# Sums over both experts of a pair in 128x64 tiles, banks in turns, and nine routing steps, in the last mixture-of-experts layer

## The chip, the cores and the metric

One core of a Trainium2 chip runs the whole program in one launch. The metric is the device time in microseconds; the median over three runs of the kernel before is 643.99 us (643.71 to 646.05). Engines are named as in the profile: PE is the matrix engine, PEld its weight load, DVE the vector engine, ACT the scalar engine, POOL the GpSimd engine, SP the engine that issues most DMAs.

## The reference

A batch of 128 images (64 x 1000) is cut into 82 overlapping patches each; a linear map and a gelu give 82 tokens of 64 channels. Two layers follow, each an attention and a mixture of experts, both with layer norm and a residual. The change is in the last mixture of experts, which has 8 experts and takes the best two of each token:

```python
logits = tokens.astype(jnp.float32) @ router_w.astype(jnp.float32).T
probs = jax.nn.softmax(logits, axis=-1)
rw, re = jax.lax.top_k(probs, TOP_K)
rw = rw / jnp.maximum(rw.sum(-1, keepdims=True), 1e-12)
combine = jnp.zeros((N, E)).at[jnp.arange(N)[:, None], re].set(rw)
out = tokens
for e in range(E):
    h = jax.nn.gelu(tokens @ w1[e] + b1[e], approximate=False)
    y = h @ w2[e] + b2[e]
    out = out + combine[:, e:e + 1] * y
```

(`tokens` is the layer norm's output; the whole layer's output is added to the residual stream `h`.)

## The kernel before

Each engine has its program written out by hand, and semaphores order them. Five stages follow each other (patches, attention, mixture of experts, attention, mixture of experts) and overlap at their seams, by hand-set turns. The last stage is `stage_moe(..., layer=1)`, with `last` true. It computes every expert for every token and weighs the results.

The batch is handled in 16 groups `g` of 8 images. A group's tokens lie transposed as `xt`: 128 partitions (64 channels of even images, 64 of odd ones) by 328 columns (4 pairs of images by 82 tokens). The 8 experts are 4 pairs `k`. One step is one `(g, k)`; what PE does in it, in this order (`step1`, from line 1704):

- `layer1` (line 1570): four f32 matmuls in 64x64 tiles for the *next* pair into the one `h1_bank`, once ACT has read the last one (`h1_ready`). ACT then applies bias and gelu over 128x656 (line 1446).
- `spread` (1580): four bf16 matmuls in 64x64 tiles, which copy the combine weights `ct` of this pair over the partitions into the one `cb_bank`. It waits for `c_ready` (ACT has made this group's `ct`) and for the last product (`hm_ready`).
- in step k=1, `logits` (1545) of group `f = g + 4`, 128*82 tiles.
- `sum_pair` (1606) of the step before: second expert matrix over the product `hm`, four f32 matmuls in 64x64 tiles. The two experts of a pair lie on partitions 0 to 63 and 64 to 127 of `hm`, and go to two different banks, `o_banks[0]` and `o_banks[1]`. For k=0 it waits until DVE has read both banks of the group before (`o_ready`).
- k=0: `finish_sum` (1617), the second bias, for group g-1. k=1: `turn_output` (1631), transposes of group g-1's sum. k=3: `turn_combine` (1559), eight bf16 transposes of the combine weights of g+1, then `turn` (1531), four transposes of the normalised tokens of g+5.

ACT's program in a step is the gelu of the next pair; after k=3's also `combine` (1439, 96x656 bf16, makes `ct` of the next group) and `copy_x` (1416, makes `xt`). DVE's program (`step(g)`, from 1901): `weigh` (1835), the product of `cb_bank` and the gelu's output, 128x656, is the last work of every step. Ahead of it come, by step, `output` (1840 and 1842: bank 0 plus `xt`, then plus bank 1), `take_logits` (1757), `residual` (1849) and the routing `route(n, k)` of a pair of groups, cut into eight pieces that the table `ROUTE` hands to the steps. The pieces are short dependent operations over 82x128: maximum, first index of the maximum, second maximum, its index, weights by tanh (on ACT, 1432), and the split of the f32 weights into three bf16 parts: three casts into `cp` (1822, 82x384) with two subtractions between (1827). POOL normalises the tokens of later groups (581 and 588) once a group's first product is there.

Layer 0's stage is the same function with `last` false. Its `sum_pair` (1608) uses 128*64 tiles: two matmuls over all 128 partitions into one bank; its `finish_sum` (1619) has 96*64 tiles.

## Time and profile before

| | us |
|---|---|
| median of 3 runs | 643.99 |
| profiled execution, its own time | 650.87 |
| profiled execution, span first to last instruction | 649.1 |
| PE busy | 586.8 (90%) |
| DVE busy | 509.4 (78%) |
| ACT busy | 297.5 (46%) |
| POOL busy | 148.9 (23%) |
| mean granted clock of PE over the span, 1 is full | 0.965 |

The busy time of an engine is the time in which at least one of its instructions runs. The last stage's steady part begins near 509 us and its last outputs are stored near 642 us. A number in a timeline row behind the start is how long the merged run of instructions lasted; as matmuls are pipelined, the start of the next row says more of what a group of them takes than its own duration does.

### The profile page before, as it was taken

The numbers are of one execution on the slowest core, as the hardware profiler recorded it, in microseconds if no ns is written. First come the engines' busy times: TensorE is split into PE (matmuls) and PEld (weight loads), VectorE is DVE, ScalarE is ACT, GpSimd is POOL, SyncE is SP. The second block draws the span as 40 slices with busy tenths as digits, with TensorE's granted clock in tenths as the row PEclk, the third lists the DMA queues.
The fourth block names the chain that finished last, engine by engine and source line by source line (L and its number), as shares of the span: only waits on it lengthen the run. The fifth ranks groups of instructions, "written<-read, shape, count | busy, mean of one in ns | idle before, by whom it ended". The sixth has DMA issues, their size and how long they took to land.

```text
span 649.1 us, 17618 instructions
## 1 busy us (share of the span) xinstructions
PE 586.8 (90%) x6943; PEld 368.7 (57%) x6943; DVE 509.4 (78%) x1524; ACT 297.5 (46%) x717; POOL 148.9 (23%) x151
## 2 busy tenths in 40 slices
PE   1999999979998999999998989999996999999983
PEld 1995565438987744444443456877774444444441
DVE  3657788985783878878878547988989999999963
ACT  0010000004442467676777638777783344545440
POOL 1000000944547204104000332415250222220000
PEclk9999999979996989999999999999996899999997
DMA  9998766210000000000000000000000001101111
GB/s 294 412 386 324 264 236 215 46 18 3 3 2 2 1 2 3 1 2 3 2 1 3 1 1 2 3 1 2 2 2 0 4 20 23 23 19 23 22 22 25
DMA packets 28898, 39.20 MB, mean 60 GB/s; under 512 B 19984, under 2 KB 20368, under 8 KB 28816
## 3 DMA queue, kind: packets, MB, share of 16 engines
q1 hardware_dynamic: 27016, 36.87, 16.6%
q10 hardware_dynamic: 1800, 1.20, 0.8%
q8 instruction: 56, 0.92, 0.6%
q14 instruction: 26, 0.21, 0.1%
HBM read 35.37 MB, written 2.69 MB: 59 GB/s over the span
## 4 chain that ended last, share of the span: by engine, by line
PE 63%; DVE 19%; issue 6%; ACT 5%; SPq 3%; DMA 2%; POOL 0%; DVEq 0%; ACTq 0%; POOLq 0%
PE bank L415 13%; PE bank L1570 8%; PE bank L1608 4%; DVE m_hm L1835 3%; PE bank L1606 3%; SPq L1223 3%; PE bank L1021 2%; PE bank L1035 2%; PE bank L1580 2%; PE bank L814 2%; PE bank L1631 2%; PE bank L1559 2%; PE bank L1591 2%; PE bank L1071 2%; PE bank L800 2%
## 5 line engine op out<-in xcount | busy, mean ns | idle before, releaser
L581 POOL TENSOR_TENSOR centred<-h,mean 82x512 f32<-82x512 f32 x64 | 72.9, 1138 | 430.9 <-DVE rstd L564 293.6
L1446 ACT ACTIVATE m_h<-bank,m_b 128x656 f32<-128x656 f32 x112 | 90.4, 807 | 104.8 <-PE bank L1570 102.6
L415 PE MATMUL bank<-cols,tok_weight 64*64 64x328 f32 (+1 forms) x1800 | 117.9, 419 | 15.3 <-DVE cols L459 14.5
L1835 DVE TENSOR_TENSOR m_hm<-bank,m_h 128x656 f32<-128x656 f32 x112 | 93.7, 836 | 27.3 <-PE bank L1580 25.9
L415 PEld LDWEIGHTS bank<-cols,tok_weight 64*64 64x64 f32 x1800 | 77.7, 139 | 51.0 <-issue 18.5
L1570 PE MATMUL bank<-m_xt,m_w 64*64 64x328 f32 x896 | 90.0, 473 | 3.3 <-ACT m_h L1446 2.6
L458 DVE COPY cols<-image 128x1992 f32<-128x1992 f32 x32 | 62.1, 1953 | 16.9 <-DMA image<-in_x_dram 14.7
L1606 PE MATMUL bank<-m_hm,m_wo 64*64 64x328 f32 x512 | 49.1, 451 | 2.6 <-DVE m_osb L1842 2.2
L980 ACT ACTIVATE sa_prob<-sa_masked,sa_low 82x82 f32<-82x82 f32 x128 | 44.6, 350 | 12.2 <-DVE sa_low L1125 12.2
L1570 PEld LDWEIGHTS bank<-m_xt,m_w 64*64 64x64 f32 x896 | 24.9, 134 | 40.1 <-issue 22.3
L392 ACT ACTIVATE tok_fm<-bank,tok_bias 128x328 f32<-128x328 f32 x16 | 7.7, 530 | 86.1 <-PE bank L415 86.1
L1453 ACT ACTIVATE m_h<-bank,m_b 128x328 f32<-128x328 f32 x96 | 45.6, 527 | 2.0 <-PE bank L1591 2.0
L1580 PE MATMUL bank<-ct,m_sel 64*64 64x328 bf16 x448 | 37.2, 313 | 6.2 <-DVE m_hm L1835 4.7
L1608 PE MATMUL bank<-m_hm,m_wo 128*64 128x328 f32 x192 | 37.1, 465 | 6.3 <-DVE m_hm L1835 6.2
L584 POOL TENSOR_TENSOR xn<-centred,rstd 82x512 f32<-82x512 f32 x32 | 35.4, 1106 | 2.5
L1591 PE MATMUL bank<-m_h,m_w 64*64 64x328 f32 x384 | 35.4, 438 | 0.0
L1580 PEld LDWEIGHTS bank<-ct,m_sel 64*64 64x64 bf16 x448 | 14.8, 106 | 36.2 <-issue 20.1
L588 POOL TENSOR_TENSOR xn<-centred,rstd 82x512 f32<-82x512 f32 x32 | 33.6, 1050 | 2.5
L464 DVE COPY h<-bank 82x512 f32<-82x512 f32 x16 | 10.3, 681 | 23.3 <-PE bank L409 23.3
L753 ACT ACTIVATE ra_xt<-bank 128x328 f32<-128x328 f32 x16 | 7.1, 443 | 43.0 <-PE bank L788 43.0
L1439 ACT ACTIVATE ct<-bank 96x656 bf16<-96x656 bf16 x32 | 22.7, 709 | 6.4 <-PE bank L1559 6.3
L858 DVE TENSOR_TENSOR h<-bank,h 82x512 f32<-82x512 f32 x16 | 10.9, 683 | 17.3 <-PE bank L814 17.3
(172 smaller groups left out, 1061.2 us busy)
## 6 DMA issues: line engine op xcount, KB each, us to landing
image<-in_x_dram SPq DMA_DIRECT2D x32, 1000.0 KB, 10.8
out_dram<-m_fin SPq DMA_DIRECT2D x16, 164.0 KB
tok_weight<-in_L_tok_weight_dram ACTq DMA_DIRECT2D x2, 400.0 KB, 8.0
m_w<-in_L_ffn_w_dram SPq DMA_DIRECT2D x2, 128.0 KB
m_sel_raw<-c_sel_dram SPq DMA_DIRECT2D x1, 256.0 KB
m_w<-in_L_ffn_expert_w_dram SPq DMA_DIRECT2D x2, 96.0 KB
m_wo<-in_L_ffn_expert_w_dram SPq DMA_DIRECT2D x4, 48.0 KB
m_sel_raw<-c_sel_dram SPq DMA_DIRECT2D x1, 192.0 KB
```

What stands on the lines that cost most here:

```text
L415: return pe.matmul(sum_bank[u % 2][s][t * D:(t + 1) * D, L * j0:L * j1], weight[s * R:(s + 1) * R, c, :], cols[u % 2][s * R:(s + 1) * R, c ...
L458: dve.tensor_copy(dst[:, :, :, 0:NBLOCK - 1], src[:, :, 0:(NBLOCK - 1) * SW].rearrange("p k (m c) -> p c k m", c=SW))
L581: pool.tensor_tensor(self.centred[:], slots(self.h, g), mean.broadcast_to([L, G, D]), ALU.subtract).then_inc(self.shifted, 1)
L980: act.activation(prob[g % 2][:, b, :], masked[g % 2][:, b, :], ACT.Exp, bias=low[g % 2][:, b:b + 1], scale=SCALE, accum_out=total[g % 2][: ...
L1446: act.activation(h1[n % RING][:], h1_bank, ACT.Gelu if last else ACT.Relu, bias=W.b1[:, k:k + 1]).then_inc(h1_ready, 1)
L1453: ins = act.activation(h2[n % RING][:, s, :], h2_bank[:, s, :], ACT.Relu, bias=W.b2[:, s, k:k + 1])
L1570: mm = pe.matmul(h1_bank[e * D:(e + 1) * D, s, :], W.w1[rows, 2 * k + e, :], xt[g % len(xt)][rows, :], start=True, stop=True)
L1580: mm = pe.matmul(cb_bank[e * D:(e + 1) * D, s, :], W.sel[rows, 128 * k + D * e:128 * k + D * e + D], ct[g % 2][rows, s:G:2, :], start=True ...
L1591: mm = pe.matmul(h2_bank[at * D:(at + 1) * D, s, :], W.w2[rows, k, :], h1[n % RING][rows, s, :], start=True, stop=True)
L1606: mm = pe.matmul(o_banks[e][cols, :], W.wo[rows, 0, k, :], hm[k][rows, s, :], start=(k == 0), stop=False)
L1608: mm = pe.matmul(o_bank[cols, 0:HALF], W.wo[:, s, k, :], hm[k][:, s, :], start=(k == 0), stop=False)
L1835: dve.tensor_tensor(hm[k][:], cb_bank, src[n % RING][:], ALU.mult).then_inc(hm_ready, 1)
```

## The change

- `sum_pair` and `finish_sum` of the last layer take both experts of a pair at once: two matmuls over 128 (96) partitions instead of four (four) over 64, into one bank. Groups take banks 4 and 5 in turns, and `sum_pair(g, 0)` waits for the output of g-2, no longer of g-1. `output` is one DVE addition instead of two.
- The routing of the last layer is a function of its own, `route_last`, in nine pieces with other places in the steps. From the second pair of groups on, the three casts of the split are made by ACT (`round_part`, in k=0, 1, 2 of odd groups) and DVE makes the two subtractions, each waiting for ACT by the semaphore `rounded`; ACT waits by `cw_ready` and `rest_ready`.
- `turn(f)` moves on PE from the end of k=3 of the group before to the end of k=0, `turn_output` from k=1 to k=2, ACT's `copy_x` from k=3 to k=0, DVE's `residual` from k=2 to k=3.

```diff
-        ROUTE = {(0, 0): (1,), (0, 1): (2,), (0, 3): (3, 4), (1, 0): (5,), (1, 1): (6, 7), (1, 3): (0,)}
-        FIRST_ROUTE = {(0, 0): (0,), (0, 1): (1, 2), (0, 3): (3, 4)}
+        ROUTE = {(0, 0): (2,), (0, 2): (3,), (0, 3): (4,), (1, 0): (5,), (1, 1): (6,), (1, 2): (7, 0), (1, 3): (1,)}
+        FIRST_ROUTE = {(0, 0): (0, 1), (0, 1): (2,), (0, 2): (3,), (0, 3): (4,)}
...
-        return g // 2 + 2 if last and r == 0 and g else (g + 2) // 2 if g % 2 == 0 else (g + 1) // 2
+        return g // 2 + 2 if last and r < 2 and g % 2 else (g + 2) // 2 if g % 2 == 0 else (g + 1) // 2
...
-        o_banks = [psum[:, 4, 0:HALF], psum[:, 5, 0:HALF]]
+        o_banks = [psum[:, 4, :], psum[:, 5, :]]
     else:
         h1_bank, cb_bank, h2_bank = psum[:, 0:2, 0:HALF], psum[:, 2:4, 0:HALF], psum[:, 6:8, 0:HALF]
         front = back = psum[:, 4, :]
-        o_bank = psum[:, 5, :]
+        o_banks = [psum[:, 5, :]] * 2
...
+        def round_part(n, i):
+            if i == 0:
+                act.wait_ge(cw_ready, n + 1)
+                act.wait_ge(c_turned, 2 * n)
+            else:
+                act.wait_ge(rest_ready, 2 * n + i)
+            act.activation(cp[:, :, :, i * EP:i * EP + E], (cw if i == 0 else rest)[:].unsqueeze(2).broadcast_to([L, 2 * G, 3, E]),
+                           ACT.Copy).then_inc(cp_ready if i == 2 else rounded, 1)
...
-                if k == COMBINE and exists(f + 1) and last:
-                    copy_x(f + 1)
+                if last:
+                    if k == 0 and g and exists(f):
+                        copy_x(f)
+                    if g % 2 and k < 3 and exists(g + 1):
+                        round_part((g + 1) // 2, k)
...
         def sum_pair(g, k):
             pe.wait_ge(hm_ready, g * NP + k + 1)
             if k == 0:
-                wait(pe, o_ready, g)
+                wait(pe, o_ready, g - 1 if last else g)
                 if g == 0 and not last:
                     pe.wait_ge(before.added, NG)
             for s in (0, 1):
                 cols = slice(s * D, (s + 1) * D)
-                if last:
-                    for e in (0, 1):
-                        rows = slice(e * D, (e + 1) * D)
-                        mm = pe.matmul(o_banks[e][cols, :], W.wo[rows, 0, k, :], hm[k][rows, s, :], start=(k == 0), stop=False)
-                else:
-                    mm = pe.matmul(o_bank[cols, 0:HALF], W.wo[:, s, k, :], hm[k][:, s, :], start=(k == 0), stop=False)
+                mm = pe.matmul(o_banks[g % 2][cols, 0:HALF], W.wo[:, 0 if last else s, k, :], hm[k][:, s, :], start=(k == 0), stop=False)
             mm.then_inc(o_pairs, 1)
         def finish_sum(g):
             for s in (0, 1):
                 cols = slice(s * D, (s + 1) * D)
-                if last:
-                    for e in (0, 1):
-                        rows = slice(e * D, (e + 1) * D)
-                        mm = pe.matmul(o_banks[e][cols, :], W.bo[rows, :], ct[g % 2][rows, s:G:2, :], start=False, stop=True)
-                else:
-                    mm = pe.matmul(o_bank[cols, 0:HALF], W.bo[0:NR, :], ct[g % 2][0:NR, s:G:2, :], start=False, stop=True)
+                mm = pe.matmul(o_banks[g % 2][cols, 0:HALF], W.bo[0:NR, :], ct[g % 2][0:NR, s:G:2, :], start=False, stop=True)
             mm.then_inc(o_done, 1)
...
                 pair_before(g, k, sum_pair)
                 if k == 0 and exists(g - 1):
                     finish_sum(g - 1)
-                if k == 1 and exists(g - 1):
+                    if exists(f):
+                        turn(f)
+                if k == 2 and exists(g - 1):
                     turn_output(g - 1)
-                if k == COMBINE:
-                    if exists(g + 1):
-                        turn_combine(g + 1)
-                    if exists(f + 1):
-                        turn(f + 1)
+                if k == COMBINE and exists(g + 1):
+                    turn_combine(g + 1)
...
+        def split(n, i):
+            at = slice(i * EP, i * EP + E)
+            if not last or n == 0:
+                if i == 0 and n == 0:
+                    dve.wait_ge(Z.pool_cleared, 7)
+                wait(dve, c_turned, 2 * n)
+                ins = dve.tensor_copy(cp[:, :, :, at], (cw if i == 0 else rest)[:].unsqueeze(2).broadcast_to([L, 2 * G, 3, E]))
+                if i == 2:
+                    ins.then_inc(cp_ready, 1)
+                else:
+                    ch(ins)
+            elif i < 2:
+                dve.wait_ge(rounded, 2 * n - 1 + i)
+            if i < 2:
+                ins = dve.tensor_tensor(rest[:], (rest if i else cw)[:], cp[:, :, 0, at], ALU.subtract)
+                if last:
+                    ins.then_inc(rest_ready, 1)
+                    dve.wait_ge(rest_ready, 2 * n + 1 + i)
+                else:
+                    ch.mark(ins)
+        def route_last(n, r):
+            src = lg[n % 2]
+            second = small[:, 2, :]
+            ch.settle()
+            if r == 0:
+                dve.wait_ge(lg_read, 2 * n + 2)
+                ch(dve.tensor_reduce(small[:, 0, :], src[:], AX_X, ALU.max))
+                ch.mark(dve.tensor_tensor(src[:], src[:], wide(small[:, 0, :]), ALU.subtract))
+            if r == 1:
+                ch.mark(dve.scalar_tensor_tensor(idx[:], src[:], 0.0, firsts, ALU.is_ge, ALU.mult))
+            if r == 2:
+                ch(dve.tensor_reduce(small[:, 1, :], idx[:], AX_X, ALU.max))
+                ch(dve.tensor_tensor(s1[:], idx[:], wide(small[:, 1, :]), ALU.is_equal))
+                wait(dve, cp_ready, n)
+                ch(dve.scalar_tensor_tensor(rest[:], s1[:], -BIG, src[:], ALU.mult, ALU.add))
+                dve.tensor_reduce(second, rest[:], AX_X, ALU.max).then_inc(exp_in, 1)
+                dve.wait_ge(exp_in, n + 1)
+            if r == 3:
+                ch(dve.tensor_tensor(idx[:], rest[:], wide(second), ALU.subtract))
+                ch(dve.scalar_tensor_tensor(rest[:], idx[:], 0.0, firsts, ALU.is_ge, ALU.mult))
+                ch.mark(dve.tensor_reduce(small[:, 1, :], rest[:], AX_X, ALU.max))
+            if r == 4:
+                ch.mark(dve.tensor_tensor(s2[:], rest[:], wide(small[:, 1, :]), ALU.is_equal))
+            if r == 5:
+                dve.wait_ge(exp_b, n + 1)
+                ch.mark(dve.tensor_scalar(small[:, 6, :], small[:, 3, :], 0.5, 0.5, ALU.mult, ALU.add))
+                ch(dve.tensor_scalar(small[:, 7, :], small[:, 3, :], -0.5, 0.5, ALU.mult, ALU.add))
+                ch.mark(dve.tensor_tensor(s1[:], s1[:], wide(small[:, 6, :]), ALU.mult))
+                ch(dve.tensor_tensor(s2[:], s2[:], wide(small[:, 7, :]), ALU.mult))
+                dve.tensor_tensor(cw[:], s1[:], s2[:], ALU.add).then_inc(cw_ready, 1)
+                dve.wait_ge(cw_ready, n + 1)
+            if r >= 6:
+                split(n, r - 6)
...
-            dve.tensor_tensor(osb[:], o_banks[0], xt[g % len(xt)][:], ALU.add).then_inc(o_even, 1)
-            dve.wait_ge(o_even, g + 1)
-            dve.tensor_tensor(osb[:], o_banks[1], osb[:], ALU.add).then_inc(o_ready, 1)
+            dve.tensor_tensor(osb[:], o_banks[g % 2][:, 0:HALF], xt[g % len(xt)][:], ALU.add).then_inc(o_ready, 1)
...
-                if k == 2 and exists(g - 1) and last:
+                if k == 3 and exists(g - 1) and last:
                     residual(g - 1)
                 for r in (FIRST_ROUTE if g == 0 else ROUTE).get((g % 2, k), ()):
                     if exists(2 * pair_of(g, r)):
-                        route(pair_of(g, r), r)
+                        (route_last if last else route)(pair_of(g, r), r)
```

In `route(n, k)` the branches for the last layer go away, and it stays as it was for layer 0. In the prologue the pieces of `route_last(0, r)` take the places of those of `route(0, k)`.

## Rows read from the trace of the kernel before

**Rows 1.** Windows: us, busy PE, PEld, DVE, ACT, POOL; granted clock; DMA share, GB/s.
```profile
480.00:520.00 40.00, 30.97 (x339) 19.82 (x334) 37.05 (x127) 18.66 (x55) 8.37 (x8) 0.79 0.01 3
...
560.00:600.00 40.00, 37.94 (x504) 19.01 (x500) 37.44 (x88) 20.36 (x31) 8.31 (x8) 1.00 0.10 22
```

**Rows 2.** Timeline of PE, one undelayed group: start us, us, line, tiles, [idle before].
```profile
589.51 0.55 PE L1559 MATMUL bank<-ident,cp 82*96 82x82 bf16 x8
589.89 0.48 PE L1531 MATMUL bank<-ident,xn 82*128 82x82 f32 x4
590.30 0.78 PE L1570 MATMUL bank<-m_xt,m_w 64*64 64x328 f32 x8
590.92 0.34 PE L1580 MATMUL bank<-ct,m_sel 64*64 64x328 bf16 x4
591.06 0.74 PE L1606 MATMUL bank<-m_hm,m_wo 64*64 64x328 f32 x8
591.61 0.34 PE L1617 MATMUL bank<-ct,m_bo 64*64 64x328 bf16 x4
592.01 0.78 PE L1570 MATMUL bank<-m_xt,m_w 64*64 64x328 f32 x8
592.61 0.32 PE L1580 MATMUL bank<-ct,m_sel 64*64 64x328 bf16 x4
592.87 0.76 PE L1545 MATMUL bank<-m_wr,m_xt 128*82 128x16 f32 x8
593.55 0.78 PE L1606 MATMUL bank<-m_hm,m_wo 64*64 64x328 f32 x8
594.27 0.64 PE L1631 MATMUL bank<-ident,m_osb 128*82 128x128 f32 x4
594.83 0.78 PE L1570 MATMUL bank<-m_xt,m_w 64*64 64x328 f32 x8
...
597.95 0.55 PE L1559 MATMUL bank<-ident,cp 82*96 82x82 bf16 x8
```

**Rows 3.** Timeline of PE: the first transposes of combine weights at full pace.
```profile
509.38 0.55 PE L1559 MATMUL bank<-ident,cp 82*96 82x82 bf16 x8
```

**Rows 4.** Timeline of all engines, from group 11 into group 12.
```profile
606.39 0.55 PE L1559 MATMUL bank<-ident,cp 82*96 82x82 bf16 x8
...
606.87 0.78 PE L1570 MATMUL bank<-m_xt,m_w 64*64 64x328 f32 x8
606.98 0.71 ACT L1439 ACTIVATE ct<-bank 96x656 bf16<-96x656 bf16 x1 [0.34 <-PE bank L1559]
...
607.74 0.34 PE L1580 MATMUL bank<-ct,m_sel 64*64 64x328 bf16 x4
...
610.06 0.78 PE L1606 MATMUL bank<-m_hm,m_wo 64*64 64x328 f32 x8 [0.55 <-DVE m_osb L1842]
...
614.46 0.55 PE L1559 MATMUL bank<-ident,cp 82*96 82x82 bf16 x8
```

**Rows 5.** Timeline of DVE and PE in group 7, while POOL normalises.
```profile
564.63 1.02 DVE L1827 TENSOR_TENSOR m_rest<-m_cw,cp 82x128 f32<-82x128 f32 x1
...
566.54 0.34 PE L1580 MATMUL bank<-ct,m_sel 64*64 64x328 bf16 x4 [0.39 <-DVE m_hm L1835]
```

**Rows 6.** Timeline of PE in layer 0: sums in 128*64 tiles and what follows.
```profile
304.12 0.77 PE L1608 MATMUL bank<-m_hm,m_wo 128*64 128x328 f32 x4
304.82 0.78 PE L1570 MATMUL bank<-m_xt,m_w 64*64 64x328 f32 x8
...
307.36 0.77 PE L1608 MATMUL bank<-m_hm,m_wo 128*64 128x328 f32 x4 [0.64 <-DVE m_hm L1835]
307.96 0.31 PE L1619 MATMUL bank<-ct,m_bo 96*64 96x328 bf16 x2
```

**Rows 7.** Groups by line, 500 to 649 us: busy us, mean ns | idle before.
```profile
L1416 ACT ACTIVATE m_xt<-bank 128x328 f32<-128x328 f32 x11 | 4.7, 431 | 0.0
...
L1842 DVE TENSOR_TENSOR m_osb<-bank,m_osb 128x328 f32<-128x328 f32 x16 | 8.0, 500 | 0.5
```

More of the change, by code:

```diff
@@ L1374, in stage_moe @@
     o_done = sem("o_done")
-    o_even = sem("o_even")
     o_ready = sem("o_ready")
@@ L1458, in output @@
             wait(act, o_turned, g)
-            act.activation(osb[:], o_bank[:, 0:HALF], ACT.Copy).then_inc(o_ready, 1)
+            act.activation(osb[:], o_banks[g % 2][:, 0:HALF], ACT.Copy).then_inc(o_ready, 1)
         act.wait_ge(prepared, W.n_prepared)
@@ L1762, in route @@
         def route(n, k):
-            src = lg[n % 2] if last else ev
             second = small[:, 2, :]
@@ L1780, in route @@
             if k == 1:
-                off = -BIG if last else -4.0
-                if not last:
-                    ch.mark(dve.reciprocal(small[:, 6, :], small[:, 5, :]))
-                ch(dve.scalar_tensor_tensor(rest[:], s1[:], off, src[:], ALU.mult, ALU.add))
-                ins = dve.tensor_reduce(second, rest[:], AX_X, ALU.max)
-                if last:
-                    ins.then_inc(exp_in, 1)
-                    dve.wait_ge(exp_in, n + 1)
-                else:
-                    ch(ins)
-                    dve.scalar_tensor_tensor(small[:, 3, :], second, -1.0, small[:, 6, :], ALU.add, ALU.mult).then_inc(exp_in, 1)
+                ch.mark(dve.reciprocal(small[:, 6, :], small[:, 5, :]))
+                ch(dve.scalar_tensor_tensor(rest[:], s1[:], -4.0, ev[:], ALU.mult, ALU.add))
+                ch(dve.tensor_reduce(second, rest[:], AX_X, ALU.max))
+                dve.scalar_tensor_tensor(small[:, 3, :], second, -1.0, small[:, 6, :], ALU.add, ALU.mult).then_inc(exp_in, 1)
                 ch.mark(dve.tensor_tensor(idx[:], rest[:], wide(second), ALU.subtract))
@@ L1802, in route @@
                 dve.wait_ge(exp_b, n + 1)
[L1803 to L1810 removed]
+                ch(dve.tensor_scalar(small[:, 5, :], small[:, 4, :], 1.0, None, ALU.add))
+                ch(dve.reciprocal(small[:, 6, :], small[:, 5, :]))
+                ch.mark(dve.tensor_tensor(small[:, 7, :], small[:, 4, :], small[:, 6, :], ALU.mult))
             if k == 4:
@@ L1815, in route @@
             if k >= 5:
[L1817 to L1827 removed]
+                split(n, k - 5)
         def weigh(g, k):
@@ L1867, in vector @@
         if last:
-            route(0, 0)
-            route(0, 1)
+            for r in range(3):
+                route_last(0, r)
             count(NG - 4)
@@ L1873, in vector @@
             yield
-            route(0, 2)
+            route_last(0, 3)
+            route_last(0, 4)
             count(NG - 3)
             take_logits(3)
-            route(0, 3)
-            route(0, 4)
+            route_last(0, 5)
             count(NG - 2)
             yield
-            for k in range(5, 8):
-                route(0, k)
+            for r in range(6, 9):
+                route_last(0, r)
             count(NG - 1)
```

30 lines of the change are left out of this document (4 added, 26 removed).

## The prediction, made before the changed kernel ran

> **What bounds the kernel now.** I read the windows first, since the change touches only the last stage. In the window 560 to 600 PE is busy 37.9 us of 40 and DVE 37.4 [rows 1]: two engines near full, so neither busy share settles anything, and the order of the waits must. So I went to the timeline of PE and took start-to-start distances. One group without a delay runs like this [rows 2]. Step k=0: expert layer (1570) to spread (1580) 0.61, spread to sum (1606) 0.14, sum to second bias (1617) 0.55, bias to the next expert layer 0.40. The last one is a wait: the expert layer has one bank, and 592.01 - 590.30 = 1.71 us is the round of matmul, gelu and matmul, which no step undercuts. Step k=1: 0.60, 0.26 into the logits, 0.68, 0.72 into the output's transposes, 0.56: 2.82 us. Step k=2 has only expert layer, spread and sum and takes the 1.71 again. Step k=3 has the same three and ends with two kinds of transposes, 0.38 us of 1559 and 0.41 of 1531. From one run of 1559 to the next pass 597.95 - 589.51 = 8.44 us [rows 2], which leaves 8.44 - 1.71 - 2.82 - 1.71 = 2.20 for k=3.
>
> The mean is longer. From the first full-pace transposes 1559, in group 0 [rows 3], to those of group 11 [rows 4], 606.39 - 509.38 = 97.01 us pass in 11 groups: 8.82 each. The excess over 8.44 is 0.38 x 11 = 4.1 us, and it is DVE's: while POOL normalises, a routing subtraction over 82x128 lasts 1.02 us, twice the 0.50 of an addition over 128x328 [rows 5, 7], the product 1835 comes late, and PE's spread idles for it ("0.39 <-DVE m_hm") [rows 5]. After group 11 no logits and tokens are left, but groups still take 614.46 - 606.39 = 8.07 us, because the sum of k=0 waits 0.55 us for DVE's second addition [rows 4]. So the stage is a PE program of 8.44 us with some DVE delay on top.
>
> **The change, part by part.**
>
> *Tiles of 128x64.* The sum keeps its columns: four quarter tiles run side by side now, two half tiles then. The nearest rows are layer 0's, where the sum has this shape already. From it to the bias of its own kind pass 0.60 us, to an expert layer in 64x64 tiles 0.70 [rows 6], where the quarter tiles take 0.55 to the bias [rows 2]. Entering costs too: from the spread into quarter tiles 0.14, into 128-row logits 0.26 [rows 2], which I take as the price of the change of shape from spread to sum. The price comes at four sums a group: +0.11 each on entering, and on leaving +0.05 to +0.15. Nothing hides it where PE has no wait. Lower bound: zero, where PE would have waited anyway; upper bound: the full 0.26 each.
>
> The Trainium skill, in "TensorEngine Tiling (Array Packing)", section Tiling Modes, says that changing the tiling mode, not just the tile, drains the engine; it speaks against this change, and rows 2 and 6 agree with it.
>
> *Fewer matmuls.* The halved count removes 8 matmuls of the sums and 2 of the bias per group. Layer 0's row with half the matmuls is no shorter (0.60 against 0.55) [rows 2, 6], so I take nothing for it.
>
> The same page, section Performance Considerations, gives each matmul an overhead of about 60 cycles. By that figure, an estimate at 2.4 GHz, 10 fewer matmuls would give back 10 x 25 ns = 0.25 us a group, 4 us in all; the rows show no such overhead where the tiles run side by side, and the sum goes by the rows.
>
> *Moved transposes.* `turn` leaves the end of k=3. Behind the transposes 1559 ACT must make `ct` (0.71 us), and the next spread starts 607.74 - 606.39 = 1.35 us after them, though PE is at its expert layer after 0.48 [rows 4]. Today the 0.38 + 0.41 us of `turn` cover this [rows 2]; without it the spread of k=0 comes 0.87 us after its expert layer instead of 0.60. This is a new wait of 0.27 us in every group; behind it stand the sum of k=3, the bias and `turn` itself.
>
> PE's new group then is:
> k=0: 0.87 + 0.26 + 0.60 (to the bias, rows 6) + 0.25 (bias to `turn`, a change of shape, as spread to logits) + 0.41 = 2.39.
> k=1: 0.60 + 0.26 + 0.68 + 0.70 = 2.24.
> k=2: 0.60 + 0.26 + 0.70 + 0.56 (output's transposes, now here) = 2.12.
> k=3: 0.60 + 0.26 + 0.70 + 0.48 = 2.04.
> Sum 8.79. All steps are above 1.71, so the gelu's round no longer costs anything. The bare program grows by 0.35 a group.
>
> *DVE's work.* A pair of groups loses two second additions (2 x 0.50) [rows 7] and three casts of 82x384; for the casts the trace rows that I show give only a bound from an addition of nearly as many columns, 0.50 each, so 1.0 to 2.5 us of some 17.6. Walk through an odd group from its expert layer at 0: PE's spreads then come at 0.87, 2.99, 5.23 and 7.35. A product starts some 0.37 us behind its spread, lasts 0.84, and the next spread needs it; the steps leave DVE 0.85 us of slack or more. In k=1 `output` waits for the bias (about 2.15) and is done by 2.6; then the subtraction waits for ACT. ACT makes `xt` when `turn` is through, 2.5 to 2.95 (0.43), then the cast. A cast on ACT isn't in the trace. Bounds: 0.43, ACT's row for 328 columns, and 0.71, its row for 656; for 384 columns a straight line between them gives 0.48 [rows 4, 7]. So the rounding is there at 3.45, the subtraction lasts 0.3 (an estimate for 128 columns without POOL: under the 0.50 of 328) to 1.0, the product of k=1 starts at 3.8 to 4.5 instead of 3.36 and is done by 4.6 to 5.35; the spread of k=2 is due at 5.23. That is no delay, or about 0.15 us in odd groups in which POOL runs beside it (1, 3, 5, 7): 0.6 us. With 0.71 for the cast it would be 0.9 more over these four. The other two roundings have slack: the gelu of k=2 ends at 4.2, the second is done near 5.0, the second subtraction at 5.7, the product of k=2 is due at 5.6, the spread behind it at 7.35. In even groups ACT isn't asked. Thus the 4.1 us of DVE delay go away, but for 0.6.
>
> *Groups 1 to 11*: 11 x 8.79 + 0.6 = 97.3 against 97.0: +0.3.
>
> *Group 0*: before 509 us the clock is at its lower level part of the time (mean 0.79 in the window 480 to 520) [rows 1], so two changes of shape, at 0.2 to 0.3 each, cost more; DVE has five operations less there. +0.4, between 0 and +0.8.
>
> *Groups 12 to 14*: no `turn`, no logits. k=0: 0.87 + 0.26 + 0.60 + 0.25 = 1.98; k=1 is bound by the gelu's round, 1.71; then 2.12 and 2.04: 7.85 against 8.07, as the sum no longer waits for the output: -0.2 x 3 = -0.6.
>
> *Group 15 and the end*: -0.2 likewise, and the last output has one addition (0.50) less in the chain: -0.7.
>
> The sum is -0.6. The profiled execution's span of 649.1 us (its own time 650.87) becomes 648.5. The median of the runs is 643.99, 1% under the profiled time; a difference this small carries over as it is: 643.4 us. A measurement of this kernel tells about 0.5% (3.2 us) from no change.
>
> **Rivals.**
>
> *Changes of shape cost nothing here* (faster). If entering and leaving the half tiles were as smooth as between quarter tiles, the new group would be shorter by 0.16 in k=0 (0.11 and 0.05), by 0.15 in k=1, and by 0.11 on entering in k=2 and k=3: 0.53 a group over 15 groups, 8 us: 635.4. For it: PE might overlap where operands allow. Against: layer 0's rows and the logits' entry. 0.08.
>
> *The waits are less than written* (faster): the new 0.27 for `ct` doesn't appear, or the halved matmuls give back something like it; 0.25 x 15 = 4: 639.5. Against it: rows 4 show the wait in the late groups, which lack `turn` already. 0.14.
>
> *The rounding's round trip makes DVE the bound again* (slower). It decides from the point at which ACT's cast takes over 0.9 us: the gelu of k=2 stands behind the first cast and the second cast behind that gelu, so the second subtraction starts at 2.95 + 0.81 + two casts, and with the next routing piece (some 0.5) and the product behind it the spread of k=3, due at 7.35, is met up to that length. A cast of 1.3 us makes each of seven odd groups 0.8 us longer, about 6 us: 649.4. For it: the output is cut into rows of 8 bf16 and the input is a broadcast. Against: ACT's rows go by the number of columns. 0.13.
>
> *DVE delays of before persist in part* (slower): the contention now falls on an operation that stands between two waits; were half of the 4.1 us left beyond my 0.6 and group 0 at its upper end, +2 in all, it would still be within 0.5%; with all of it left, 643.4 + 3.5 + 0.4 = 647.3, over the bound. 0.10.
>
> *My forecast*, little or no change: 0.55, its own range 641 to 646.5.
>
> **How the numbers follow.** Likeliest 643.4. To leave out no more than 2 in 10, the range takes in the wait rival and most of the slower ones: 639.5 to 648. Faster by over 0.5% (under 640.8): 0.08 + 0.12 and a little of the forecast's own spread = 0.22. Slower (over 647.2): 0.20. Same: 0.58.
>
> **What the changed profile would show.** The start-to-start distances: spread to sum 0.25, sum to expert layer 0.70, transposes 1559 to spread 1.35 in every group; a group of about 8.8 us from 1 to 11 and 7.85 after; ACT's cast near 0.48; hardly any "DVE m_hm" ahead of the spread; DVE's share in these windows down from 37 to 33 or 34 of 40 us. I would be wrong if sum and neighbours overlapped, if the cast took over 1 us, or if PE still waited for the product of k=1 or k=2.

## The result, and the profile after

The changed kernel is slower by 0.76%: a median of 650.86 us (646.98 to 653.87, 20 runs) against 646.91 us (642.72 to 651.21, 20 runs), a ratio of 1.0076 (95% 1.0055 to 1.0097). The ratio, which is taken between runs on the same chip, makes it 4.9 us, the two medians 4.0. The three runs of the kernel before that were shown ahead of the prediction lie in the lower part of its scatter, and their median is 2.9 us under that of the twenty. By the ratio, "no change" was wrong, and the time is above the range.

| | before | after |
|---|---|---|
| profiled execution, its own time, us | 650.87 | 651.66 |
| span, us | 649.1 | 649.9 |
| PE busy, us | 586.8 | 592.2 |
| DVE busy, us | 509.4 | 496.8 |
| ACT busy, us | 297.5 | 307.5 |
| mean granted clock of PE | 0.965 | 0.973 |

PE works 5.4 us more, DVE 12.6 less. The windows that answer to [rows 1]:

```profile
480.00:520.00 40.00, 31.23 (x284) 16.88 (x287) 35.61 (x120) 18.70 (x45) 6.34 (x7) 0.79 0.02 4
...
560.00:600.00 40.00, 39.08 (x400) 17.82 (x398) 33.03 (x76) 22.16 (x35) 8.33 (x8) 1.00 0.08 19
```

From 560 to 600 DVE falls from 37.4 to 33.0 us and PE rises from 37.9 to 39.1 (second and fourth numbers). That is what was forecast, and it tells nothing of the loss, which is in what waits for what.

The timeline of PE in group 11 and into group 12, no delays in it; it answers to [rows 2, 4] (start, duration, line):

```profile
598.91 0.55 PE L1572 MATMUL bank<-ident,cp 82*96 82x82 bf16 x8
599.39 0.78 PE L1583 MATMUL bank<-m_xt,m_w 64*64 64x328 f32 x8
600.26 0.34 PE L1593 MATMUL bank<-ct,m_sel 64*64 64x328 bf16 x4
600.53 0.77 PE L1616 MATMUL bank<-m_hm,m_wo 128*64 128x328 f32 x4
601.13 0.31 PE L1622 MATMUL bank<-ct,m_bo 96*64 96x328 bf16 x2
601.38 0.50 PE L1544 MATMUL bank<-ident,xn 82*128 82x82 f32 x4
601.81 0.78 PE L1583 MATMUL bank<-m_xt,m_w 64*64 64x328 f32 x8
...
604.05 0.78 PE L1583 MATMUL bank<-m_xt,m_w 64*64 64x328 f32 x8
...
606.17 0.78 PE L1583 MATMUL bank<-m_xt,m_w 64*64 64x328 f32 x8
606.78 0.32 PE L1593 MATMUL bank<-ct,m_sel 64*64 64x328 bf16 x4
607.03 0.77 PE L1616 MATMUL bank<-m_hm,m_wo 128*64 128x328 f32 x4
607.73 0.55 PE L1572 MATMUL bank<-ident,cp 82*96 82x82 bf16 x8
...
615.59 0.55 PE L1572 MATMUL bank<-ident,cp 82*96 82x82 bf16 x8
```

(In the changed kernel's file the lines have moved: 1583 is the expert layer, 1593 the spread, 1616 the sum, 1622 the second bias, 1572 and 1544 the transposes of the combine weights and of the tokens, 1870 DVE's product, 1779 its subtraction.) The four steps, from one expert layer to the next and for k=3 over the transposes too, are 601.81 - 599.39 = 2.42, 604.05 - 601.81 = 2.24, 606.17 - 604.05 = 2.12, and 8.82 less these three = 2.04. Predicted were 2.39, 2.24, 2.12 and 2.04. A late group takes 615.59 - 607.73 = 7.86 (7.85 predicted).

The same start-to-start reading over the whole last stage, for both kernels (all in us; a group goes from one run of the transposes of combine weights to the next; "ahead" is from the last matmul of the attention (line 1021) to the first of these transposes; "end" is from the last of them to the start of the last residual addition):

| | ahead | group 0 | groups 1 to 11 | of them undelayed | groups 1, 3, 5, 7, 9 | 12 to 14, each | end | sum |
|---|---|---|---|---|---|---|---|---|
| before | 25.16 | 10.24 | 97.01 | 8.44 | 9.83, 9.18, 9.07, 9.54, 8.62 | 8.07 | 10.91 | 167.5 |
| after | 25.41 | 10.87 | 100.78 | 8.82 | 9.98, 9.62, 9.63, 9.40, 9.19 | 7.86 | 10.09 | 170.7 |

The undelayed group grew by 0.38 (0.35 predicted), but five odd groups are still longer than 8.82: 1.16 + 0.80 + 0.81 + 0.58 + 0.37 = 3.72 us where I had 0.6. That is the miss.

### The profile page after: what moved, and what is told of

The parts are those of the page before. It is cut to its first block, busy times and chain, and to the rows that moved or that the text cites. A ratio compares the mean times of both kernels' runs of the same rounds, so it can differ in the third digit from the quotient of the medians.

```text
span 649.9 us, 17050 instructions
## 1 busy us (share of the span) xinstructions
PE 592.2 (91%) x6655; PEld 363.8 (56%) x6655; DVE 496.8 (76%) x1487; ACT 307.5 (47%) x738; POOL 148.9 (23%) x151
## 4 chain that ended last, share of the span: by engine, by line
PE 69%; DVE 16%; ACT 5%; issue 4%; SPq 3%; DMA 2%; POOL 0%; DVEq 0%; ACTq 0%; POOLq 0%
PE bank L415 13%; PE bank L1616 10%; PE bank L1583 9%; PE bank L1593 3%; PE bank L1634 3%; SPq L1223 3%; DVE m_hm L1870 2%; PE bank L1021 2%; PE bank L1035 2%; PE bank L814 2%; PE bank L1604 2%; PE bank L1572 2%; PE bank L1071 2%; PE bank L800 2%; PE bank L1029 2%
## 5 line engine op out<-in xcount | busy, mean ns | idle before, releaser
L1616 PE MATMUL bank<-m_hm,m_wo 128*64 128x328 f32 x448 | 87.7, 470 | 6.7 <-DVE m_hm L1870 6.5
L980 ACT ACTIVATE sa_prob<-sa_masked,sa_low 82x82 f32<-82x82 f32 x128 | 44.6, 350 | 12.6 <-DVE sa_low L1125 12.6
L1616 PEld LDWEIGHTS bank<-m_hm,m_wo 128*64 128x64 f32 x448 | 22.3, 136 | 30.7 <-issue 15.3
L1071 PEld LDWEIGHTS bank<-v,pt 128*82 128x82 f32 x256 | 21.6, 157 | 4.4 <-issue 1.6
```

The lines of the kernel that those rows point to most:

```text
L980: act.activation(prob[g % 2][:, b, :], masked[g % 2][:, b, :], ACT.Exp, bias=low[g % 2][:, b:b + 1], scale=SCALE, accum_out=total[g % 2][: ...
L1616: mm = pe.matmul(o_banks[g % 2][cols, 0:HALF], W.wo[:, 0 if last else s, k, :], hm[k][:, s, :], start=(k == 0), stop=False)
```

## Experiments

Each kernel computes the reference; nothing is left out in any of them. Ratios are to the kernel before, with 95% intervals. As the times of one kernel turned out to scatter by 7 to 8.5 us, the verdict on each term rests on the stage's own distances. In the repeats the distances from group 2 on come back within some hundredths; in the kernel before, groups 0 and 1 move by 0.4 and the part ahead of them by 1.0.

**Repeats.** How far do the stage's distances repeat, and does the loss lie in them?

> The kernel before itself, for a second trace. Theory: groups 1 to 11 take 97.0 us and the stage 167.5, within 0.3 us. Rival: the stage varies by more, and the 1.7 us between the stages' difference (3.2) and the medians' (4.9) lies there.

> The changed kernel itself, for a second trace. Theory (the last stage's length is fixed by the program, the scatter of the runs lies before it): groups 1 to 11 take 100.8 us and the stage 170.7 again, within 0.3 us, while the end of the attention before it lies anywhere between 468 and 475 us. Rival (the last stage itself varies, by the clock, by some us between executions): stage outside 170.4 to 171.0.

> The kernel before, a third trace, with the same expectations: stage 167.5, or up to 2 us more ahead of group 0 if the clock falls earlier.

> The changed kernel, a third trace, with the same expectations: stage 170.7, or, if the clock falls earlier than in the first trace, up to 2 us more ahead of group 0, as in the two experiments in which it fell at 479 us.

| | time | groups 1 to 11 | sum of the stage |
|---|---|---|---|
| before again | 650.28, 645.2 | 97.13, 96.70 | 167.8, 166.8 |
| after again | 650.86, 653.66 | 100.75, 100.75 | 170.7, 170.7 |

The changed kernel's stage repeats as expected. That of the kernel before came out at 166.8 once, outside the 0.3 us around 167.5 that were expected, by its part ahead of group 0 (24.42 instead of 25.16). The stage's difference is 170.7 - 167.4 (mean of three) = 3.3 us. The times say 4.0 by the medians and 4.9 by the ratio (3.6 to 6.3 by its interval). The 0.7 to 1.6 us between is not located: the code of the earlier stages is the same, and over all traces of the study the end of the attention falls anywhere from 467.9 to 474.5 us. In the six traces here it goes with PE's granted clock between 200 and 240 us: 0.86, 0.87 and 0.96 in the kernel before, with the attention's end at 474.0, 473.1 and 469.1 us; 0.94, 0.95 and 0.87 in the changed one, with 470.7, 469.9 and 472.7.

**The transposes of the tokens back at the end of k=3** (changed kernel, one part undone).

```diff
                     finish_sum(g - 1)
-                    if exists(f):
-                        turn(f)
...
+                if k == COMBINE:
+                    if exists(g + 1):
+                        turn_combine(g + 1)
+                    if exists(f + 1):
+                        turn(f + 1)
```

(ACT's `copy_x(f + 1)` goes back to k=3 with it.)

> The changed kernel with the token transposes back at the end of k=3 and ACT's copy of them back in k=3; all else as changed. Theory (my prediction's account of PE, plus DVE's odd groups at the size the trace now shows): the undelayed group falls from 8.82 to about 8.45 us, since the transposes again cover the 0.27 us in which ACT makes the combine weights and one change of shape goes away; over groups 1 to 11 that is 4 us. ACT's first cast then no longer stands behind the copy, so the odd groups' excess of 3.7 us should shrink as well, to 0 to 2 us. In all 4 to 7 us faster than the changed kernel, 0 to 2 us faster than the kernel before. Rival (the loss is the half tiles' changes of shape alone): the undelayed group stays over 8.7 us and the time within 1 us of the changed kernel's.

Ratio 1.0041 (1.001 to 1.0072), groups 1 to 11 in 96.98, undelayed 8.43. The move costs 0.39 in every group, near the price that the prediction gave it (the new wait 0.27 and a change of shape). The odd groups kept 4.28 us of excess; I had expected it to shrink to 0 to 2. Timeline of DVE, POOL and PE in group 3:

```profile
531.90 1.04 POOL L581 TENSOR_TENSOR centred<-h,mean 82x512 f32<-82x512 f32 x1 [6.27 <-DVE m_hm L1871]
...
532.13 0.96 DVE L1780 TENSOR_TENSOR m_rest<-m_cw,cp 82x128 f32<-82x128 f32 x1
...
533.02 1.04 POOL L588 TENSOR_TENSOR xn<-centred,rstd 82x512 f32<-82x512 f32 x1
...
533.13 0.97 DVE L551 TENSOR_SCALAR tmp<-tmp 82x32 int32<-82x32 int32 x1
...
535.33 0.34 PE L1593 MATMUL bank<-ct,m_sel 64*64 64x328 bf16 x4 [0.69 <-DVE m_hm L1871]
```

ACT's cast is early now (it ends at 531.97, before DVE is through with the output), and still two DVE operations are long. Each begins inside one of POOL's two instructions and ends as that one does: 533.09 and 532.94, 534.10 and 534.06. An operation of 0.18 us (551) took 0.97. So the lateness isn't ACT's; DVE is stopped by POOL, twice, as a piece of the layer norm's scale (551 and 552) stands behind the subtraction. (DVE computes this scale for the later groups in six pieces of two or three short operations, which the table `SCALE_MINE` hands to steps as `(group, k)`; POOL waits for the last piece before it normalises these groups.)

**The scale's pieces moved from k=1 of groups 1, 3, 5 to that of 2, 4, 6** (changed kernel).

```diff
-{(1, 1): 1, (2, 3): 1, (3, 1): 1, (4, 3): 1, (5, 1): 1, (6, 3): 1}
+{(2, 1): 1, (2, 3): 1, (4, 1): 1, (4, 3): 1, (6, 1): 1, (6, 3): 1}
```

> The changed kernel with the three pieces of the layer norm's scale that DVE runs in k=1 of groups 1, 3 and 5 moved to k=1 of groups 2, 4 and 6. Theory: these pieces, which my walk through an odd group left out, stand between the subtraction and the product of k=1 and are late in full: groups 1, 3 and 5 get 0.43 us shorter each, 1.3 us in all (0.2% of the time, at the edge of what the runs can tell, so read from the trace). Rival (the odd groups wait for ACT's cast and for POOL's contention alone, and the pieces lie in slack): groups 1, 3, 5 keep their 9.98, 9.62 and 9.63 us.

Groups 1 to 11 in 98.81, group 1 at 8.88, groups 3 and 5 at 9.19: 1.97 us less in the three, where 1.3 was expected. (The ratio, 1.0107 with 1.0059 to 1.0154 from four runs, doesn't resolve 2 us.) Without the move, in the changed kernel's group 3, timeline of ACT, POOL, DVE and PE:

```profile
529.11 0.51 ACT L1443 ACTIVATE cp<-m_cw 82x384 bf16<-82x384 f32 x1
...
529.65 1.04 POOL L588 TENSOR_TENSOR xn<-centred,rstd 82x512 f32<-82x512 f32 x1
529.72 1.12 DVE L1779 TENSOR_TENSOR m_rest<-m_cw,cp 82x128 f32<-82x128 f32 x1 [0.88 <-ACT cp L1443]
...
530.87 0.18 DVE L551 TENSOR_SCALAR tmp<-tmp 82x32 int32<-82x32 int32 x1
...
531.08 0.18 DVE L552 TENSOR_SCALAR tmp<-tmp 82x32 int32<-82x32 int32 x1
...
531.30 0.84 DVE L1870 TENSOR_TENSOR m_hm<-bank,m_h 128x656 f32<-128x656 f32 x1
...
532.28 0.34 PE L1593 MATMUL bank<-ct,m_sel 64*64 64x328 bf16 x4 [0.60 <-DVE m_hm L1870]
```

and after it:

```profile
528.62 1.12 DVE L1779 TENSOR_TENSOR m_rest<-m_cw,cp 82x128 f32<-82x128 f32 x1 [0.88 <-ACT cp L1443]
...
529.77 0.84 DVE L1870 TENSOR_TENSOR m_hm<-bank,m_h 128x656 f32<-128x656 f32 x1
...
530.76 0.34 PE L1593 MATMUL bank<-ct,m_sel 64*64 64x328 bf16 x4 [0.17 <-DVE m_hm L1870]
```

PE's wait falls from 0.60 to 0.17, by 551 and 552 (531.30 - 530.87 = 0.43). Group 1 gains more, 1.10, as there the piece's first operation was stopped itself, for 1.01 us. Timeline of POOL and DVE in the changed kernel:

```profile
511.58 1.04 POOL L588 TENSOR_TENSOR xn<-centred,rstd 82x512 f32<-82x512 f32 x1
...
511.68 1.01 DVE L544 SCALAR_TENSOR_TENSOR tmp<-stats 82x32 f32<-82x32 f32 x1
```

The pieces stood in DVE's program between the subtraction and the product of k=1, and the prediction's walk left them out.

**POOL started two products later, after that of k=2** (changed kernel): the subtraction then has no POOL beside it.

```diff
-                pool.wait_ge(hm_ready, NP * (f - FRONT - 2) + 1)
+                pool.wait_ge(hm_ready, NP * (f - FRONT - 2) + 3)
```

> The changed kernel with POOL's normalisation released by the third product of the group instead of the first, so that it runs in k=3 and the next k=0. Theory (in k=1 of odd groups POOL's running instruction blocks the short DVE operation): the first subtraction takes 0.28 us instead of 1.12, and even with the scale piece between, the product of k=1 is in time; groups 3, 5 and 9 fall to 8.83, unless the blocking shows again in k=3 or k=0, where the short operations of pieces 4, 1, 2 and 5 stand: then even groups rise above 8.83 too, as in the run with POOL earlier (9.37). Groups 1 to 11 between 98 and 100 us in the first case, over 101 in the second. Rival (ACT's round trip): nothing changes in k=1, groups 3, 5, 9 stay within 0.1 us.

Groups 1 to 11 in 98.92 (-1.9); group 9 is down to 8.82, the undelayed length; ratio 1.004 (1.0012 to 1.0068). The same point of group 3, timeline of DVE:

```profile
527.59 0.29 DVE L1779 TENSOR_TENSOR m_rest<-m_cw,cp 82x128 f32<-82x128 f32 x1 [0.47 <-ACT cp L1443]
...
528.33 0.84 DVE L1870 TENSOR_TENSOR m_hm<-bank,m_h 128x656 f32<-128x656 f32 x1
```

0.29 instead of 1.12: what it lasted beyond 0.29 was POOL. What is left in groups 1, 3, 5 and 7 (0.68, 0.43, 0.17 and 0.58) was not followed piece by piece.

**POOL started one product earlier** (changed kernel).

```diff
-                pool.wait_ge(hm_ready, NP * (f - FRONT - 2) + 1)
+                pool.wait_ge(hm_ready, NP * (f - FRONT - 2))
```

> The changed kernel with POOL's normalisation released by the last product of the group before instead of the first product of the group, about 2 us earlier, so that it has ended or nearly ended when DVE makes the first subtraction in k=1 of an odd group. Theory (the excess of the odd groups is POOL's contention with that subtraction, 1.12 us against 0.28): the first subtraction is under 0.5 us long, odd groups lose 0.4 to 0.8 us each from 1 to 9, 2 to 3 us in all, unless the contention only moves to the five short operations of k=0, which have about 0.5 us of slack. Rival (the excess is the round trip to ACT, 0.88 us of idle DVE): the odd groups change by under 0.2 us each.

Worse: ratio 1.0117 (1.0075 to 1.0159), groups 1 to 11 in 104.73, even groups at up to 9.37 too. POOL meets two routing operations in k=0 now, timeline of POOL and DVE:

```profile
534.92 1.04 POOL L581 TENSOR_TENSOR centred<-h,mean 82x512 f32<-82x512 f32 x1 [6.89 <-DVE m_hm L1870]
535.01 1.10 DVE L1801 TENSOR_TENSOR m_s<-m_idx,m_small 82x128 f32<-82x128 f32 x1
536.04 1.04 POOL L588 TENSOR_TENSOR xn<-centred,rstd 82x512 f32<-82x512 f32 x1
536.15 1.09 DVE L1804 SCALAR_TENSOR_TENSOR m_rest<-m_s,m_lg 82x128 f32<-82x128 f32 x1
```

Two stops of 0.8 each in a row. In group 7 (11.71) the granted clock fell to its lower level as well (0.50, or 1.2 GHz, from 569 to 571 us, after PE had worked only 0.98 of the 2 us from 565 to 567), so about 2 us of the 4 are the clock's; that is an estimate from the other odd groups, which have at most 10.01.

**The casts back on DVE** (changed kernel). Would the stage be shorter without ACT's round trip, the slower rival on record?

```diff
-            if not last or n == 0:
+            if True:
...
-                    if g % 2 and k < 3 and exists(g + 1):
-                        round_part((g + 1) // 2, k)
```

(The third piece returns to (1, 2) of `ROUTE`.)

> The changed kernel with the three casts of the split made by DVE again (first cast and subtraction in k=1, second cast, subtraction and third cast in k=2 of odd groups) and none by ACT. Theory (the odd groups are late because short DVE operations last until POOL's running instruction ends, not for the round trip to ACT): DVE does 1.1 to 2.5 us more in odd groups and gets none of the waits back, so odd groups become longer by 0.3 to 1.5 us each from 1 to 9: stage 1.5 to 6 us longer than the changed kernel's 170.7. Rival (the round trip, 0.88 us of idle DVE in each odd group, is the cause): odd groups fall by 0.4 us or more and the stage is under 169.5.

Groups 1 to 11 in 103.39, 2.6 more; ratio 1.0113 (1.008 to 1.0145). At this placement ACT's casts help. With them on DVE both are stopped, timeline of DVE and POOL:

```profile
527.54 1.03 DVE L1769 CAST cp<-m_cw 82x384 bf16<-82x384 f32 x1
...
528.44 1.04 POOL L588 TENSOR_TENSOR xn<-centred,rstd 82x512 f32<-82x512 f32 x1
528.61 1.02 DVE L1775 TENSOR_TENSOR m_rest<-m_cw,cp 82x128 f32<-82x128 f32 x1
```

**Quarter tiles back** (changed kernel with 64x64 tiles, two banks, two additions and the wait for the output of the group before, all else as changed).

```diff
-                mm = pe.matmul(o_banks[g % 2][cols, 0:HALF], W.wo[:, 0 if last else s, k, :], hm[k][:, s, :], ...)
+                    for e in (0, 1):
+                        rows = slice(e * D, (e + 1) * D)
+                        mm = pe.matmul(o_banks[e][cols, 0:HALF], W.wo[rows, 0, k, :], hm[k][rows, s, :], ...)
```

> The changed kernel with the sums back in 64x64 tiles, two banks for the two experts, the second addition and the wait for the group before's output; its order of steps and its nine routing pieces stay. Theory (the changes of shape cost what the prediction's sum has): the undelayed group falls from 8.82 to about 8.3 us, 0.5 x 11 = 5 to 6 us over groups 1 to 11; groups 12 to 14 stay near 7.9 since the sum of k=1 waits for the output again; the end is 0.5 us longer. In all 4 to 6 us faster than the changed kernel, so level with the kernel before or a little faster. Rival (half tiles cost nothing that PE would not wait for anyway): undelayed group above 8.7 us, time within 1 us of the changed kernel's or slower for the second addition.

Groups 1 to 11 in 94.76 (-6.0), undelayed 8.22 (-0.60), late groups 7.66; ratio 0.9977 (0.9948 to 1.0005). In this order of the steps the half tiles cost 0.60 a group, in k=0 to 3 by 0.16, 0.09, 0.20 and 0.15; the rest of the change, without them, gains 2.2 us over these groups (97.01 to 94.76). The late groups were expected at 7.9, with a wait for the output again.

**Half tiles alone** (kernel before, with the sums of the changed one).

```diff
-            dve.tensor_tensor(osb[:], o_banks[0], xt[g % len(xt)][:], ALU.add).then_inc(o_even, 1)
-            dve.wait_ge(o_even, g + 1)
-            dve.tensor_tensor(osb[:], o_banks[1], osb[:], ALU.add).then_inc(o_ready, 1)
+            dve.tensor_tensor(osb[:], o_banks[g % 2][:, 0:HALF], xt[g % len(xt)][:], ALU.add).then_inc(o_ready, 1)
```

> The kernel before with the half tiles alone: sums in 128x64 tiles, banks in turns, one addition for the output, the wait for the output two groups back; its routing pieces and the order of its steps stay. Theory (half tiles cost PE the change of shape only in steps that PE itself bounds): k=0 and k=2 stay hidden in the gelu's round of 1.71 us, k=3 grows by 0.15 to 0.16, k=1 keeps its 2.82, so the undelayed group goes from 8.44 to 8.60; groups 12 to 14 take 7.86 instead of 8.07, the end is 0.7 us shorter; DVE has one addition less and its delays of 4.1 us shrink by 0 to 2. The last stage is 167.5 us in the trace of before; it should be 166 to 168 here. Rival (the half tiles cost their full 0.37 a group wherever they stand): undelayed group 8.8 us, stage 170.

Ratio 1.0018 (0.9992 to 1.0045), groups 1 to 11 in 98.26, undelayed 8.58: the same tiles cost 0.14 a group here. Timeline of PE:

```profile
585.20 0.78 PE L1570 MATMUL bank<-m_xt,m_w 64*64 64x328 f32 x8
...
586.91 0.78 PE L1570 MATMUL bank<-m_xt,m_w 64*64 64x328 f32 x8
...
589.72 0.78 PE L1570 MATMUL bank<-m_xt,m_w 64*64 64x328 f32 x8
...
591.43 0.78 PE L1570 MATMUL bank<-m_xt,m_w 64*64 64x328 f32 x8
```

k=0 and k=2 (586.91 - 585.20, 591.43 - 589.72) still take the 1.71 us of the gelu's round, which swallows the changes of shape there. In the changed kernel both steps carry more work and last longer than 1.71, and nothing swallows them.

**Without the parts that cost.** From these results: transposes of the tokens back in k=3, the scale's pieces in k=3 or in even groups; once with half tiles, once with quarter tiles. The edits are those above, and

```diff
-{(1, 1): 1, (2, 3): 1, (3, 1): 1, (4, 3): 1, (5, 1): 1, (6, 3): 1}
+{(2, 1): 1, (2, 3): 1, (3, 3): 1, (4, 1): 1, (4, 3): 1, (5, 3): 1}
```

> The changed kernel with the token transposes back at the end of k=3 (as in the run that had only that, undelayed group 8.43) and the six scale pieces in k=1 and k=3 of groups 2 and 4 and k=3 of groups 3 and 5, so that they are done before group 6. Theory (what is left of the odd groups' excess is scale pieces that POOL stretches to 0.97 us in k=1, and POOL's unusual second start in group 6 and 7, which waits for the last scale piece): odd groups 3, 5 and 7 fall from 9.3 to 9.4 to under 8.6, groups 1 to 11 take 93 to 94.5 us, the stage 163 to 165. Rival (the excess is POOL against the subtraction alone): groups 3, 5, 7 stay above 9.0.

> The same as the half-tile kernel of this call but with the sums in 64x64 tiles, two banks and two additions. Theory (change of shape costs PE in each step): undelayed group 8.04 to 8.1 us against 8.43 with half tiles; groups 12 to 14 near 7.7; groups 1 to 11 take 89 to 91 us, the stage 160 to 162, which makes the whole 5 to 7 us faster than the kernel before (ratio 0.989 to 0.992). Rival (DVE, with a second addition per group again, becomes the bound once PE is shorter): odd groups over 8.8 us and the stage above 163.

With half tiles: ratio 0.9966 (0.9937 to 0.9995), groups 1 to 11 in 93.10; group 7, too, is at the undelayed 8.43. With quarter tiles: 0.9893 (0.9857 to 0.9928), groups 1 to 11 in 88.45, undelayed 7.97. A repeat:

> The same kernel as c1_quarter_best, once more with more rounds, to narrow the interval of its ratio to the kernel before: 0.986 to 0.992 expected from a last stage 9.1 us shorter (9.1 of 646 is 1.4%) and from the first measurement, 0.9893.

0.984 (0.9805 to 0.9875), a median of 637.34 us, the best kernel of the study. One group of it, timeline of PE:

```profile
580.34 0.55 PE L1573 MATMUL bank<-ident,cp 82*96 82x82 bf16 x8
...
581.13 0.78 PE L1584 MATMUL bank<-m_xt,m_w 64*64 64x328 f32 x8
...
582.84 0.78 PE L1584 MATMUL bank<-m_xt,m_w 64*64 64x328 f32 x8
...
584.99 0.73 PE L1584 MATMUL bank<-m_xt,m_w 64*64 64x328 f32 x8
...
586.91 0.78 PE L1584 MATMUL bank<-m_xt,m_w 64*64 64x328 f32 x8
...
588.32 0.55 PE L1573 MATMUL bank<-ident,cp 82*96 82x82 bf16 x8
```

Its steps are 1.71, 2.15, 1.92 and 2.20; before, with the output's transposes in k=1, they were 1.71, 2.82, 1.71 and 2.20 [rows 2]. On PE the only difference left is `turn_output`: its move to k=2, out of the step of the logits, gives 0.67 in k=1 and costs 0.21 in k=2, 0.46 a group.

**The scale's pieces moved in the kernel before**, and **POOL later in the quarter-tile kernel**.

> The kernel before with only its six scale pieces moved to k=1 and k=3 of groups 2 and 4 and k=3 of groups 3 and 5. Theory (the scale pieces are part of the lateness of odd groups before the change too, and POOL's second start in groups 6 and 7 waits for the last of them): group 7 falls from 9.54 to about 9.1 and group 1 by 0.4 or more; groups 3 and 5 gain in k=1 and may lose in k=3, where five routing operations stand already; groups 1 to 11 take 94.5 to 96.5 us instead of 97.0. Rival (the delays before come from the routing with its casts alone): within 0.3 us of 97.0.

> The fastest kernel so far (quarter tiles, token transposes at the end of k=3, scale pieces moved; groups 1 to 11 in 88.5 us, stage 158.4) with POOL released by the third product. Theory: its odd groups have no excess left but 0.66 us in group 1, so a later POOL can only shift the blocking to other places: 88 to 90 us for groups 1 to 11, the time level within 0.5%. Rival (there is hidden blocking even in the undelayed groups): below 87.5 us.

In the kernel before the move is worth 0.7 us (groups 1 to 11 in 96.34; 0.9986, 0.9955 to 1.0016): groups 1, 3, 5 and 7 get shorter, 2, 4 and 6 longer (8.85, 9.35, 9.04), which have pieces in them now or in the last step of the group before. In the quarter-tile kernel the late POOL is a loss, 93.74 against 88.45 (0.9918, 0.9885 to 0.9951), where I had expected no more than 90. Timeline of POOL, DVE and PE: it now stops the scale's piece in k=3.

```profile
523.19 1.11 POOL L588 TENSOR_TENSOR xn<-centred,rstd 82x512 f32<-82x512 f32 x1
523.31 1.03 DVE L548 SCALAR_TENSOR_TENSOR tmp<-tmp 82x32 f32<-82x32 f32 x1
...
525.59 0.34 PE L1594 MATMUL bank<-ct,m_sel 64*64 64x328 bf16 x4 [0.67 <-DVE m_hm L1882]
```

## Why the prediction was wrong, step by step

*PE's new group*: right, step by step (8.82 against 8.79), and each term was undone on its own: the moved transposes -0.39, the half tiles -0.60 (the rival that took them as free had 0.53, from [rows 6]). Within the 0.60 two shares were off and made up for each other: 0.09 in k=1 and 0.20 in k=2, where that rival had 0.15 and 0.11. The fewer matmuls gave nothing that shows.

*Group 0*: +0.63, or +0.36 to +0.79 against the three traces of before; within the bounds, +0.4 taken. *Groups 12 to 14*: -0.63 in all, -0.6 predicted. *End*: -0.82, -0.7 predicted. *Ahead of group 0*, where I had no term: +0.25, but the kernel before itself varies there from 24.42 to 25.46.

*ACT's casts*: 0.51 us against the 0.48 from the straight line. The subtraction behind the first cast starts 3.48 us after the group's expert layer (584.85 - 581.37 in group 9; 3.45 predicted). Groups by line, 500 to 650 us (busy us, mean ns | idle ahead):

```profile
L1443 ACT ACTIVATE cp<-m_rest 82x384 bf16<-82x384 f32 x14 | 7.2, 517 | 2.7 <-DVE m_rest L1779 2.6
...
L1779 DVE TENSOR_TENSOR m_rest<-m_cw,cp 82x128 f32<-82x128 f32 x7 | 5.6, 799 | 3.8 <-ACT cp L1443 3.8
...
L1779 DVE TENSOR_TENSOR m_rest<-m_rest,cp 82x128 f32<-82x128 f32 x7 | 1.9, 279 | 0.3 <-ACT cp L1443 0.3
```

The first subtraction's mean of 799 ns stands beside 279 for the second, the same work: one runs beside POOL and the other doesn't.

*The failed step* is "Thus the 4.1 us of DVE delay go away, but for 0.6". 3.72 us stay. The walk through an odd group was right up to the rounding and wrong in what followed it:

- It had left out the pieces of the layer norm's scale that `SCALE_MINE` puts into k=1 of groups 1, 3 and 5, between subtraction and product: 1.97 us (measured by moving them).
- It had the stopped subtraction at 1.0 us; it takes 1.12, and from the product to PE's spread pass 0.99, not the 0.84 of the product alone. 3.48 + 1.12 + 0.03 + 0.99 = 5.62 against a spread due at 2.42 + 2.24 + 0.60 = 5.26: 0.36 of delay, not 0.15, and in groups 3, 5 and 9: 1.1 us. A later POOL took all of it away in group 9, which the walk left out of the groups "in which POOL runs beside it (1, 3, 5, 7)". (Group 1 keeps 0.06.)
- Group 7, 0.58: the last piece of the scale, (6, 3), lets POOL begin an additional pair of instructions in it, and both pairs meet DVE (564.06 for 1.13 and 566.90 for 1.00). The two half-tile kernels with the transposes back in k=3 differ in the scale's pieces alone: group 7 takes 9.40 in the one and the undelayed 8.43 in the other.

With the 3.72 in place of the 0.6, the sum is -0.6 + 3.1 = +2.5; the two profiled stages differ by 3.2 (170.7 - 167.5). Between them lie 0.4 of the undelayed groups, 0.2 of group 0, the 0.25 ahead of it, and -0.15 of late groups and end. The rival that took place is "DVE delays of before persist" (chance 0.10); its own price with all of them left, 3.5 + 0.4 us less the 0.6 of the sum, is 3.3 us over the kernel before, as the stages' difference is. Its weight was too small for a reason that can be read: the contention was seen in [rows 5] and then only its size on one operation was asked for, not what else stood in the same stretch of DVE. The rival of ACT's round trip is refuted: its condition was a cast of over 0.9 us, and the cast takes 0.51. Also, in the half-tile kernel without the parts that cost, which keeps ACT's casts, groups 2 to 11 have no excess (8.42 or 8.43 each). The stage with DVE's casts, 2.6 us longer, says only that there they are stopped too.

Also off was the base: 643.99 is a median of three runs from a scatter of 642.7 to 651.2. The same -0.6 from the median of twenty would have said 646.3, still 4.6 us short. "A measurement of this kernel tells about 0.5%" holds for the twenty runs, whose interval is 0.2% to either side; the median of three was itself off by 0.45%. One slip changes nothing: from expert layer to spread the prediction reads 0.61 where [rows 2] give 0.62.

## What to carry to other kernels

A walk through an engine's program must list every operation that the tables put there, those of neighbouring work (here a layer norm's scale) included; with one piece missing, a walk that ends within some tenths of a microsecond of its deadline comes out wrong. Judge an order of steps by which of them are held up by a floor (here the gelu's round of 1.71 us): work and changes of tile shape are free there and cost in full elsewhere, so the same tiles cost 0.14 in one order and 0.60 in another. And what POOL stops on DVE depends on where POOL's instructions fall: here 12.6 us less work on DVE left 3.7 of 4.1 us of delay, while moving three small pieces of the scale took away 2.0.
